# A Mamba-style scan block with a quantised FFN on one core: the FFN's row tile laid over two scan periods, and its up product made by ScalarE and GpSimd

## The reference

```python
x1 = einsum(in_proj_w, ctx); u = silu(causal_conv4(x1) + conv_b)
dt, B, C = split(x_proj_w @ u); delta = softplus(dt_proj_w @ dt + b)
state = state * exp(delta * A) + (delta * u) * B      # 16 states per channel, over 512 steps
y = (sum_n(state * C) + D * u) * silu(layernorm(x))
x = x + tanh(g_xattn) * y
def linear_bit(x, w, g):                              # act_quant: 127 / row maximum
    return act_quant(rmsnorm(x, g)) @ ternary_quant(w).T
n = layernorm(x)
h = silu(linear_bit(n, w1, g1)) * linear_bit(n, w2, g2)   # 2048 hidden columns
x = x + tanh(g_ffn) * linear_bit(h, w3, g3)
```

## Time and profile before

| what | us |
|---|---|
| median of 3 runs | 931.42 (929.79 to 937.34) |
| the profiled execution: device time | 939.2 |
| its span, first to last instruction | 936.7 |

### The profile page before, as it was taken

The page is one execution under the profiler, slowest core; times in us unless marked ns, Lnnn a source line. Parts: engine busy times, 40 slices in busy tenths (PEclk is TensorE's granted clock), DMA queues, the critical chain, the costliest instruction groups (busy, mean ns, idle before and its releaser), DMA issues.

```text
span 936.7 us, 7751 instructions
## 1 busy us (share of the span) xinstructions
PE 629.2 (67%) x2258; PEld 234.7 (25%) x2258; DVE 715.1 (76%) x873; ACT 522.4 (56%) x750; POOL 470.2 (50%) x229
## 2 busy tenths in 40 slices
PE   6436647586678686858685867767676756656775
PEld 3101113333233132313131312222222212222332
DVE  2389786898786979797888788788989798854552
ACT  3577735645557556464747474646564656344552
POOL 1054534344274748473747466474757475643422
PEclk9756767777677797878788787868686869787897
DMA  3699613427420102043101111233111110000000
GB/s 86 137 341 275 218 29 119 129 67 230 143 90 23 35 10 53 6 131 74 45 24 35 33 35 34 62 98 79 34 34 34 35 34 23 1 11 11 13 12 22
DMA packets 38553, 68.06 MB, mean 73 GB/s; under 512 B 10816, under 2 KB 13376, under 8 KB 36336
## 3 DMA queue, kind: packets, MB, share of 16 engines
q1 hardware_dynamic: 38512, 67.57, 25.2%
HBM read 46.32 MB, written 4.46 MB: 54 GB/s over the span
## 4 chain that ended last, share of the span: by engine, by line
PE 35%; DVE 30%; ACT 12%; issue 11%; DMA 9%; SPq 2%; POOL 0%; POOLq 0%; ACTq 0%; DVEq 0%
DVE hb L910 12%; DVE dbu_ps L901 8%; PE ring L1304 8%; PE y_ps L1284 8%; PE ring L1359 7%; PE du_ps L1273 6%; DMA x<-in_L_ffn_w_dram 4%; DMA dl_rep<-delta 3%; ACT dA L676 3%; PE ring L1222 2%; DMA h<-in_L_ffn_w_dram 2%; PE y_ps L1295 2%; DVE u L856 2%; SPq L393 1%; PE ring L1348 1%
## 5 line engine op out<-in xcount | busy, mean ns | idle before, releaser
L540 POOL TENSOR_TENSOR hb<-hb,c_rep 128x2048 f32<-128x2048 f32 x64 | 289.6, 4525 | 315.3 <-DVE hb L910 306.8
L910 DVE TENSOR_TENSOR_SCAN hb<-dA,dbu_ps 128x1024 f32<-128x1024 f32 x128 | 291.8, 2280 | 8.8 <-ACT dA L676 3.7
L1273 PE MATMUL du_ps<-du,sel_q 32*128 32x512 f32 x128 | 103.0, 895 | 220.5 <-DVE dbu_ps L901 220.4
L676 ACT ACTIVATE dA<-dl_rep,a_neg 128x511 f32<-128x511 f32 x256 | 161.9, 709 | 15.4 <-DMA dl_rep<-delta 12.3
L901 DVE TENSOR_TENSOR dbu_ps<-du_ps,b_rep 128x1024 f32<-128x1024 f32 x128 | 157.0, 1226 | 6.1 <-PE du_ps L1273 3.9
L1284 PE MATMUL y_ps<-hb,sel_s 128*32 128x512 f32 x512 | 142.7, 709 | 0.0
L1273 PEld LDWEIGHTS du_ps<-du,sel_q 32*128 32x128 f32 x128 | 25.1, 243 | 260.5 <-issue 251.9
L525 POOL TENSOR_TENSOR h<-h,g3b 128x1024 f32<-128x1024 f32 x24 | 55.9, 2352 | 66.2 <-ACT work L740 66.2
L687 ACT ACTIVATE h<-ring,deq 128x512 f32<-128x512 f32 x48 | 33.0, 687 | 100.1 <-PE ring L1304 100.1
L1359 PE MATMUL ring<-w3T,hT 128*128 128x512 fp8e4 x256 | 75.6, 462 | 5.8 <-issue 4.6
L1304 PE MATMUL ring<-w2T,a12T 128*128 128x512 fp8e4 x256 | 71.0, 403 | 10.9 <-DVE h L925 10.9
(11 more groups left out here) (140 smaller groups left out, 916.4 us busy)
## 6 DMA issues: line engine op xcount, KB each, us to landing
dl_rep<-delta SPq DMA_DIRECT2D x256, 64.0 KB, 2.0
h<-in_L_ffn_w_dram SPq DMA_DIRECT2D x12, 1024.0 KB, 5.5
x<-in_L_ffn_w_dram SPq DMA_DIRECT2D x12, 1024.0 KB, 6.2
xt<-in_x_dram SPq DMA_DIRECT2D x16, 256.0 KB, 3.5
b_rep<-bc_scratch SPq DMA_DIRECT2D x16, 256.0 KB, 4.5
c_rep<-bc_scratch SPq DMA_DIRECT2D x16, 256.0 KB, 5.6
x<-in_x_dram SPq DMA_DIRECT2D x4, 1024.0 KB, 7.4
out_dram<-x SPq DMA_DIRECT2D x16, 256.0 KB, 2.3
```

The source lines that it names most:

```text
L540: g.tensor_tensor(hb[:, s % 4, :, :], hb[:, s % 4, :, :], c_rep[:, :, :], ALU.mult)\
L676: ins = a.activation(dA[:, s % 2, i, 1:L], dl_rep[:, s % 2, 1:L], ACT.Exp, scale=a_neg[:, s % 16, i:i + 1])
L910: v.tensor_tensor_scan(hb[:, s % 4, 2 * half:2 * half + 2, :].rearrange("p a l -> p (a l)"), dA[:, s % 2, 2 * half:2 * half + 2, :].rearra ...
L1273: mm(du_ps[:, :], sel_q[rows, :], du[rows, k % 2, :], start=True, stop=True).then_inc(du_bc, 1)
```

## The change

The arithmetic is the same. What moves:

- **Up product.** In the periods ScalarE copies each up chunk out of PSUM, scaled, into the new tile `up_sb` (`scale_up`, 48 copies of 128x512), and GpSimd multiplies it into h, half a row tile at a time (`times_up`, 24 of 128x1024). VectorE's `mul_up` (L925) stays for tiles 12 to 15 alone. All four `gate_up` chunks of a tile now stand in q = 3 of its first period, with `bcast_du` behind the first.
- **Places.** `gated_y` stands behind the first scan of q = 1 and no longer ahead of it. `in_proj` and `tap` of tile k+5 move from q = 2 to q = 0, and the three `conv_tap`s from the end of q = 2 to ahead of the first scan of q = 1. `square_sum` and `h_gain` move to q = 0, `hidden_max` to q = 1, `quant_scales` to q = 2, `transpose_hidden` and `down` to q = 2, `output` to q = 3 of the same period, `sum_states(2k)` from q = 2 to q = 3, `skip_term` out of it into q = 1. SiLU of the gate z and of u go to q = 3.
- **Weights.** Three chunk buffers (h, the second x1 buffer, up_sb), the loads a step earlier, the first passes in the pattern 0, 2, 2, 3, 3, 2 chunks a step. The loads of x1 and the gains are issued later. x1 has two buffers, refilled a row tile at a time (`reload_x1`).
- **End.** The last `times_c` runs on VectorE (`last_times_c`), so do the two gains of tile 12 (`tail_gains`). The rows of tiles 13 to 15 have buffers of their own, so their normalisation can stand ahead. ScalarE's and VectorE's orders are interleaved more finely, and `hidden_max` and `hidden_scales` of a tile stand ahead of the next tile's `mul_up`s.

```diff
 LAG_F, LAG_G, LAG_O = ET, ET + 1, ET + 2
 TAIL = KQ - LAG_F
 NB = 4
-XB = 3
+XB = 2
...
 def abs_chunks(s):
 
-    return [2 * s, 2 * s + 1] if s < WCH // 2 else []
+    first = (0, 0, 2, 4, 7, 10, WCH)
+    return range(first[s], first[s + 1]) if s + 1 < len(first) else []
...
         def chunk_buf(j):
 
-            return x1[:, 2, :, :] if j % 2 else h[:, :].rearrange("p (t d) -> p t d", t=4)
+            if j % WB == 1:
+                return x1[:, 1, :, :]
+            return (h, None, up_sb)[j % WB][:, :].rearrange("p (t d) -> p t d", t=4)
...
-                if j >= WCH + 2:
-                    filled(sp, ("wT", j - WCH - 2, 3))
+                if WB <= j < WCH + WB:
+                    sp.wait_ge(w_abs, j - WB + 1)
+                if j >= WCH + WB:
+                    filled(sp, ("wT", j - WCH - WB, 3))
...
-                    if q == 1 and k >= LAG_O:
-                        store_out(k - LAG_O)
+                    if q == 0 and k >= LAG_O and k + 2 < NT:
+                        reload_x1(k + 2)
+                    if q == 3 and k >= LAG_G:
+                        store_out(k - LAG_G)
                     for c in abs_chunks(s):
-                        load_chunk(c + 2)
-                    if TERN_AT < s < TERN_AT + WCH - 1:
-                        load_chunk(s - TERN_AT + WCH + 1)
+                        load_chunk(c + WB)
...
+            def times_up(ft, i):
+
+                half = slice(H // 2 * i, H // 2 * (i + 1))
+                pool.wait_ge(silu_done, 4 * ft + 2 * (i + 1))
+                pool.wait_ge(up_done, 4 * ft + 2 * (i + 1))
+                g.tensor_tensor(h[:, half], h[:, half], up_sb[:, half], ALU.mult).then_inc(h_pool, 1)
...
                         times_c(s - 1)
+                    if q == 3 and f >= 0:
+                        times_up(f, 0)
+                    if q == 0 and gt >= 0:
+                        times_up(gt, 1)
+                        h_gain(gt, 0)
+                        h_gain(gt, 1)
                     if q == 1:
+                        if gt >= 0:
+                            hidden_rstd(gt)
+                        if k + 1 < KQ:
+                            mul_du(k + 1)
                         z_rstd(k)
-                        if gt >= 0:
-                            h_gain(gt, 0)
-                            h_gain(gt, 1)
-                            hidden_rstd(gt)
                         if f >= 0:
                             row_rstd(f)
-                    if q == 2:
-                        if k + 1 < KQ:
...
+            def scale_up(ft, c):
+                job = ("up", ft, c)
+                filled(act, job)
+                if c == 0 and ft >= 1:
+                    act.wait_ge(h_pool, 2 * ft)
+                a.activation(up_sb[:, 512 * c:512 * c + 512], bank(job)[:, :], ACT.Copy,
+                             scale=deq[:, ft % 4, 1:2]).then_inc(up_done, 1)
...
+                    if q == 0 and k + AHEAD < KQ and f >= 0:
+                        tap(k + AHEAD)
+                    if s + 1 < Q * KQ:
+                        exps(s + 1)
+                    if q == 0 and g >= 0:
+                        square_sum(g, 0)
+                    if q == 0:
+                        if f < 0:
+                            tap(k + AHEAD)
+                        if g >= 0:
+                            square_sum(g, 1)
+                        if et == ET - 1 and b + 1 < B:
+                            xproj_evac(b + 1)
+                    if q == 1:
+                        if k + 1 < KQ:
+                            softplus(k + 1)
+                        if g >= 0:
                             quant_hidden(g)
-                    if q == 3:
...
-                    if q == 3 and f >= 0:
-                        evac_aT(f)
+                    if q == 3:
+                        if f >= 0:
+                            for c in range(4):
+                                gate_silu(f, c)
+                                scale_up(f, c)
+                        silu_z(k)
+                        if k == 0:
+                            silu_u(ET)
+                        if k + AHEAD < KQ:
+                            silu_u(k + AHEAD)
+                        if k + 1 < KQ:
+                            a.preload_act_table_set(EXP_LN)
...
+            def last_times_c():
+
+                s = Q * KQ - 1
+                dve.wait_ge(scan_done, 2 * (s + 1))
+                dve.wait_ge(ld_c, 64 * B)
+                v.tensor_tensor(hb[:, s % 4, :, :], hb[:, s % 4, :, :], c_rep[:, :, :], ALU.mult).then_inc(hc_last, 1)
 
...
                     add_input(s, 0)
-                    if q == 0 and o >= 0:
-                        output(o)
+                    if q == 1:
+                        if ahead:
+                            taps = mark(conv_tap(k + AHEAD, 1))
+                        if ahead:
+                            after(taps)
+                            taps = mark(conv_tap(k + AHEAD, 2))
+                        if ahead:
+                            after(taps)
+                            conv_tap(k + AHEAD, 3).then_inc(conv_done, 1)
+                    if q == 2:
+                        if f >= 0:
+                            row_bias(f)
+                        if g >= 0:
+                            evac_hT(g)
+                    if q == 3 and g >= 0:
+                        output(g)
+                    scan(s, 0)
                     if q == 1 and k >= 1:
                         gated_y(k - 1)
-                    if q == 2 and g >= 0:
-                        max0 = hidden_max(g, 0)
-                    if q == 3 and f >= 0:
-                        quant_scales(f)
-                    scan(s, 0)
...
-                    if q == 0:
-                        if g >= 0:
-                            mul_up(g, 0)
-                        after(st)
-                        st = mark(v.bn_aggr(zmv[:, :], zst[:, :]))
-                    if q == 2 and g >= 0:
-                        max1 = hidden_max(g, 1)
+                    if q == 1 and g >= 0:
+                        ss = square_total(g)
+                        hidden_max(g, 0)
+                        after(ss)
+                        mean_square(g)
+                        top = hidden_max(g, 1)
+                    if q == 1 and f >= 0 and k + 1 < KQ:
+                        lost_digits(k + 1)
+                    if q == 2:
+                        z_bias(k)
+                        if f >= 0:
+                            quant_scales(f)
...
+                    scan(s, 1)
+                    if q == 1:
+                        if f >= 0 and k + 1 < KQ:
+                            log1p(k + 1)
+                        dve.wait_ge(ld_xt[k % 2], 16 * (k // 2 + 1))
+                        st = mark(v.bn_stats(zst[:, :], xt[:, k % 2, :]))
+                        if g >= 0:
+                            after(top)
+                            hidden_scales(g)
+                        after(st)
+                        st = mark(v.bn_aggr(zmv[:, :], zst[:, :]))
+                        if k >= 1:
+                            add_scan(k - 1)
+                        after(st)
+                        z_var(k)
+                        if f < 0:
+                            lost_digits(k + 1)
+                            log1p(k + 1)
+                        if f >= 0:
+                            link(row_stats(f))
+                            link(row_aggr(f))
+                            row_var(f)
...
                     if q == 0:
-                        if g >= 0:
-                            gate_up(g, 2)
                         bcast_du(s + 1)
-                        if g >= 0:
-                            gate_up(g, 3)
+                        if k + AHEAD < KQ:
+                            in_proj(k + AHEAD)
+                        if et == ET - 1 and b + 1 < B:
+                            x_proj(b + 1)
                         if k >= 1:
                             sum_states(2 * k - 1)
...
+                        bcast_du(s + 1)
+                        skip_term(k)
                     if q == 2:
-                        if k + AHEAD < KQ:
-                            in_proj(k + AHEAD)
-                        bcast_du(s + 1)
-                        sum_states(2 * k)
                         if g >= 0:
                             transpose_hidden(g)
+                            down(g)
+                        bcast_du(s + 1)
+                    if q == 3 and et == 2 and b + 2 < B:
+                        ctx_transpose(b + 2)
+                    transpose_w(s)
+                    if q == 2 and f >= 0:
+                        transpose_rows(f)
                     if q == 3:
-                        if et == 2 and b + 2 < B:
-                            ctx_transpose(b + 2)
+                        sum_states(2 * k)
+                        if f >= 0:
+                            gate_up(f, 0)
                         if s + 1 < Q * KQ:
```

(10 more changed lines are left out.)

430 lines of the change are left out of this document (201 added, 229 removed).

## The result

The changed kernel takes 858.76 us (median; 856.71 to 860.85) where the kernel before, timed beside it, took 933.81 us: a ratio of 0.920, 95% interval 0.915 to 0.925. The forecast was 870 us, -61 us; it is -75 us. That lies in the band of 845 to 890 us, to which the prediction gave 0.60. The profiled execution has a span of 854.9 us (before 936.7). One of the four runs of the kernel of experiment 8 took 1034.76 us at a granted TensorE clock of 0.56, where its others have 0.79, and is left out.

What follows compares the result with a forecast made beforehand. VectorE's instructions in their order, plus waits ahead of each, were taken to bound the middle stage. Middle -37, weights' stage -17 and tail -7 gave -61 us off the 931.42 us median: 870 us; 845 to 890 (0.60), 838 to 902 (8 in 10).

Steps and rivals of the forecast that it cites:

- The layout with cheap TensorE values: Middle stage: periods of 45.2 us with `in_proj`, 41.7 without; dear values 48.9 and 45.6; forecast a third between.
- Term 1, the up product: Middle stage: taking `mul_up` off VectorE shortens a period's instructions by 1.5 us, 16.5 us over eleven periods.
- Term 2, `output`: Middle stage: `output` stands 7 us behind the end of `down`, so its 30.9 us of waits go.
- Term 2, `down` "even, no room": Middle stage: `down` ends at 35.3, the q = 3 broadcast at 37.4 us, just when VectorE arrives.
- Term 2, `conv_tap`: Middle stage: new VectorE wait of 2.2 to 3.3 us in six periods, 13 us at the low end.
- Term 2, `gated_y`: Middle stage: the 1.7 us wait goes in periods with `in_proj`; 1.3 us is left in others.
- the rival of a slow TensorE: All TensorE operations dear: periods 48.9 and 45.6 us, middle stage 527, total 897 us; chance 0.17.
- The hidden row: Middle stage: VectorE waits 0.9 us at the second maximum and is 1.0 us early for the softplus.
- the rival on the other side: GpSimd's order becomes the bound through late `times_c`; 9 us of lateness gives 953 us; chance 0.06.
- Term 3, weights' stage: Earlier loads remove 18.4 us, `gated_y` waits 9.5, first broadcasts 2; `conv_tap` waits add 13: -17 us.
- Term 4, tail: After the middle stage: `times_c` on VectorE, earlier last sum, shorter `gate_up` loop: -7 us, bounds 0 and -18.
- The shared port: Tail: `last_times_c` and `tail_gains` could each wait out a GpSimd product, the sum up to 5 us higher.

Runs made afterwards that it cites:

- experiment 8: Changed kernel with the weights' stage loads as before (two chunk buffers, old queue order): 870.99 us, ratio 0.932.
- (1): Kernel before with only the up product of tiles 2 to 10 moved to ScalarE and GpSimd: 928.54 us, ratio 0.993.
- (2): Kernel before with that up product moved and `gated_y` behind the first scan of q = 1: 928.37 us, ratio 0.991.
- (3): Kernel before with `output` one scan later in q = 0: 911.57 us, ratio 0.975.
- (4): Changed kernel with q = 3's broadcast ahead of the hidden row's transposes and `down`, and `evac_hT` later in q = 2: 912.56 us, ratio 0.976.
- (7): Changed kernel with TensorE matmuls of zeros: ahead of the sum without `in_proj`, 854.85 us; less there, more ahead of transposes and `down`, 849.95 us.
- experiment 10: Changed kernel with the last `times_c` on GpSimd, as before: 864.06 us, ratio 0.924.
- 9: Changed kernel with the `conv_tap`s of periods 1 to 3 behind the second scan of q = 1: 872.03 us, ratio 0.933.

## Why the prediction was right, and where not

The total was near, and in part by luck. Stage by stage the saving was 20 us more (middle), 7 less (weights) and 7 more (tail) than forecast, and inside the middle stage two errors of 11 us cancel. The profiled executions, from which the stages are taken, are 82 us apart and the medians 75: the one before lay 5 us above its median and the one after 2 below.

*The bound.* VectorE's order sets the period: right, and more so after (433 of 480 us).

*The middle stage as a whole.* The forecast has two parts: instructions with their small gaps, 6 x 41.2 + 5 x 39.0 = 442 us, and 58 us of waits. Measured are 444 us (480.0 less the 35.6 us of named waits) and 36 us. The same split of the kernel before is 462 and 75 us, so the first part fell by 17.9 us, where the sum had 16.5. The error is in the waits. The layout with cheap TensorE values, 6 x 45.2 + 5 x 41.7, gives 480 us, which is what was measured. What I added to it is too much: 14 us for a third of the way to the dear values, and 6 us for k = 7 and 11 and the ragged ends (these two periods took 44.5 and 42.5 us, the mean of their kind being 44.0 and 43.2). That the cheap layout fits is luck: it has 11 us too much ahead of `conv_tap` and 11 us too little ahead of `gated_y`, see below.

*Term 1, the up product (-16.5 us).* VectorE's busy time fell by 23 us in the stage, which is 17.9 with the gaps. But alone it is worth 5 to 7 us (1), because in the kernel before ScalarE's chain through q = 0 ends just behind it (2). That chain has no term in the prediction, which let `gated_y`'s wait stand for it. The change of place of `gate_up` and the silus, which I had counted as nothing, took it out of q = 0; that it is what freed the rest was read from the traces, not tried alone.

*Term 2, `output` (-30.9 us).* Right: cover alone gives 22 of them (3).

*Term 2, `down` "even, no room".* Right that there was none: `down` took 6.3 us, not 4.3, and VectorE waits 7.4 us for `du_ps`, which I had named as a sign of error. But the prediction costed the order at nothing; next to the one with the broadcast ahead it is worth 53 us, `evac_hT`'s place included (4).

*Term 2, `conv_tap` (+13 us).* Mis-sized, 11 us too much. I took 3.6 us for `in_proj` from the earlier trace rows, a row at a granted clock of 0.54, and it took 1.98 at 1.00, so that the wait was 0.3 to 0.7 us in a period: 2.0 us in all instead of 13.

*Term 2, `gated_y` (1.3 us left).* Mis-sized, 11 us too little: 17.8 us where five times 1.3 were laid out. It is up to 4.0 us in the periods without `in_proj`, since without that work TensorE idles, and the sum behind runs at a granted clock of 0.57 (7). The two errors have opposite signs. One price level for all periods, "a third of the way from cheap to dear", was the wrong form: periods with `in_proj` took 44.0 us, less than the cheap layout (45.2), those without 43.2, between cheap and dear (41.7 and 45.6). So the rival of a slow TensorE came true in single places (`down` and the sum of these periods) and not as a whole.

*The hidden row.* 0.7 us ahead of the second maximum, 0.8 ahead of softplus: as laid out (0.9, 1.0). `times_c` of q = 3 ends 8.6 us into the period (forecast 8.3, limit 10), so the rival on the other side did not come about.

*Term 3, weights' stage (-17, was -10).* The loads are right in kind (8), and the wait ahead of `gated_y` fell by 8.3 us (forecast 9.5). The `conv_tap`s wait 9.5 us instead of 13. The term that is missing in the sum: VectorE is busy 4.5 us longer. Timeline, changed kernel, VectorE and GpSimd at the fourth of the twelve `tern`s, and one `tern` from another place:

```profile
132.44 1.28 DVE L1153 TENSOR_SCALAR x<-x,w_inv 128x2048 f32<-128x2048 f32 x1
...
154.53 4.51 POOL L576 TENSOR_TENSOR hb<-hb,c_rep 128x2048 f32<-128x2048 f32 x1
156.22 3.91 DVE L1153 TENSOR_SCALAR h<-h,w_inv 128x2048 f32<-128x2048 f32 x1
```

Three `tern`s (156.22, 203.82, 255.17) are issued while a `times_c` runs on GpSimd. Each takes 3.9 us instead of 1.28 and ends 1.1 us behind the `times_c`: 7.9 us in all. Before, all twelve took 1.25 to 1.29 us, and nine of them waited for a load first. But there one of seven tiny instructions on 128x3 elements, which read two tensors in SBUF, met a `times_c`: the seven took 5.64 us together, in the changed kernel 1.34. First VectorE, then GpSimd, kernel before:

```profile
190.08 5.64 DVE L993 SCALAR_TENSOR_TENSOR at<-at 128x3 f32<-128x3 f32 x7
```
```profile
190.00 4.51 POOL L540 TENSOR_TENSOR hb<-hb,c_rep 128x2048 f32<-128x2048 f32 x1 [5.72 <-DVE hb L910]
```

So some 4.3 of the 7.9 us were lost before the change too, and the collisions make up 3.6 of the 7 us that are missing; another 2.6 stand in VectorE's waits for ScalarE's softplus (7.6 us instead of 5.0). The three `tern`s are not chance: they are the fourth, eighth and twelfth, each in q = 2, and the same three take 3.9 us in every other run with the early loads. With the old loads (8) only the twelfth does. That the waits for loads keep the others clear of `times_c` was not tested by itself.

*Term 4, tail (-7, was -14).* Step by step: last scan to `gated_y` 6.9 instead of 12.9 us (-6, forecast -5; experiment 10 shows 5 us of it for the place of `times_c`, for which I had 2); from there to `gate_up` of tile 12 21.4 instead of 20.6 (+0.8, forecast +1.4); tile 12 to 13 8.6 instead of 14.4 (-5.8, and I had said that it stays); 13 to 14 to 15 -0.2 and -2.9 (forecast -5 for both); the end -0.4 (forecast +2). The step that I had wrong is tile 12 to 13: with row buffers of their own the tiles behind are normalised and quantised while tile 12 is in `gate_up` (ScalarE does it for tile 13 at 771.30 and 781.41 us), which I did not lay out. Part of it is only an earlier start: tile 13's `gate_up` then stands still for 4.1 us, for VectorE, which frees its bank. So 12 to 14 taken together is the fairer reading, -6.0 us where -2.5 were forecast.

*The shared port.* `last_times_c` took 2.29 us (estimate 2.5); the two `times_up`s beside it took 6.19 us together instead of 4.7, so GpSimd lost 1.5 us. In the Trainium skill, "SBUF — State Buffer", section "Who interferes with whom", VectorE and GpSimd exclude each other for a two-input instruction, and also for a `tensor_scalar` that uses both ports; the trace agrees with both: `last_times_c` and the 128x3 instruction above have two inputs, and a `tern` is such a `tensor_scalar` (2048 columns in 1.28 us, where the two-input product of as many takes 2.29). The second, for which I had not looked, cost more (7.9 us) than the first.

## What to carry to other kernels

A wait is worth removing only if nothing else ends just behind it: price a part by asking what the engine would wait for next (1, 2, 9), on every engine's queue. A sum can be right because its errors cancel: check each term against its own row, also when the total fits. Fill a gap of TensorE with work that waits for nothing rather than leave it idle: the order of `down` and a broadcast, with the evacuation behind it, decided 53 us, and filler of zeros gave another 9. Take the duration of a matmul from a row with the same work in front of it, not from the same operation elsewhere; prices taken at the wrong clock made the two largest errors here, 11 us each.

## What the runs showed of the hardware

- A sum of sixteen matmul records took 3.6 us behind steady work (granted clock 1.00, that is 2.4 GHz) and 6.3 us after 2.5 us idle (0.57, mostly 1.2 GHz); filler of the same form in front brought it back to 3.6 us (1.00).
- Matmuls of 32 columns for different 32 partitions overlap when they alternate: 130.6 us for all sums, 183.7 us one step after the other.
- A VectorE `tensor_scalar` of 128x2048 in SBUF stood still as long as a GpSimd product ran (1.28 to 3.9 us), and so did a two-input one of 128x3 (seven of them 5.6 us instead of 1.3). In the tail, where VectorE's product began first, GpSimd lost the time (4.7 to 6.2 us). In the profile such time is busy time, not a wait.
